# Routed experts computed on sorted 128-row tiles in place of all experts for all tokens

## The chip, the cores and the metric

The kernel runs on one core of a Trainium2 chip. The metric is the device time of one execution in microseconds. Several executions are timed and one is profiled: the profile gives, for each instruction on each engine, its start, its length and what ended the wait before it.

## The reference

x has 2048 tokens of 256 features. Two layers act on it. Layer 0 is attention (16 heads of 16 over all 2048 tokens) and a mixture of experts; layer 1 is a small attention over the first 32 tokens' scores and one binarised 256x256 product. Each of the four sub-blocks is a LayerNorm, a modulation and a gated residual. The part that the change concerns is the mixture of experts:

```python
    x = hidden_states.reshape(-1, h)                      # 2048 x 256
    probs = softmax(x @ router_w.T)                       # 8 experts
    topk_w, topk_idx = top_k(probs, 2)
    topk_w = topk_w / sum(topk_w)
    combine = zeros((T, 8)).at[arange(T)[:, None], topk_idx].add(topk_w)
    for gw, uw, dw, ce in zip(gate_w, up_w, down_w, combine.T):   # 256x176, 256x176, 176x256
        moe_out += ce[:, None] * (silu(x @ gw) * (x @ uw) @ dw)
    shared = silu(x @ s_gate_w + s_gate_b) * (x @ s_up_w + s_up_b) @ s_down_w + s_down_b   # 352 wide
    return moe_out + shared
```

Only two of the eight weights `ce` of a token are not zero.

## The kernel before

Five engines run streams of their own, in the order in which their instructions are written, and wait on semaphores. Every product in the mixture of experts is made of three passes over numbers split in a rounded high part and a rest (fp32r): high by high, high by low, low by high. Products of layer 1 and all transposes are in full fp32.

First come the LayerNorm and the projections. Then attention runs as 16 units (`unit`, L519) of 16 key tiles each: a chunk of 512 queries and a group of four heads. Beside the last two units run the second LayerNorm of chunks 0 to 2, its transposes (`turn1`, L634) and the router (`logits` L642, `router` L1322). Chunk 3 follows inside the first chunk of the next stage.

The mixture of experts (`chunk`, L743, L1060, L1400) computes every expert for every token. The 8x176 expert columns and the 352 shared columns lie side by side: 1760 columns, NI = 14 tiles of up to 128. For each of four chunks of 512 tokens and each of the 14 tiles, a step does the following. PE makes gate and up products (`hidden`, L719, 6 matmuls of 512 columns each, L725). For the 11 expert tiles it also spreads the combine weights over 128 rows with a selector (L760). ACT takes Silu (L1067), DVE multiplies by up and by the combine weight (L1409, L1414), ACT rounds (L1075), DVE makes the rest (L1416), and PE makes 12 down matmuls of 256 columns (`down`, L701, L713), which sum over all 14 tiles in two PSUM banks. DVE multiplies the sum by the gate row in `gate_sums` (L1424), and Pool adds it to x (L1848). The layer 1 work of chunk c-1 runs beside the steps of chunk c (`beside_second`, `beside_rest`): LayerNorm on DVE and Pool, transposes, products in `l1_attend` (L855) and `l1_feed` (L884), and adds on DVE (`add_product`, L1499). Chunk 3's layer 1 work is the end of the kernel, in two halves of 256 tokens (L923 to L950, L1609 to L1670). PE is in strict order, so everything beside a step lengthens it by what PE spends on it.

SP issues nearly all DMAs: weights of the experts are loaded during attention (`load_gate_up`, L326), outputs at the end. Pool issues none.

## Time and profile before

| | us |
|---|---|
| median of 3 runs | 1183.8 (1178.45 to 1184.11) |
| profiled execution | 1180.42 |
| its span, first to last instruction | 1178.6 |
| PE busy in the span | 1090.2 (92%) |
| DVE, ACT, POOL busy | 885.8 (75%), 666.9 (57%), 245.6 (21%) |
| granted TensorE clock, mean | 0.968 of full speed |

The page divides the span in 40 slices and gives each engine's busy share, then names the chain of work that ended last. It is read first for the order of the stages, then stage by stage: an engine that is busy all the time in a stage is what a change has to relieve there, and the chain of waits in it says whether another one interrupts it.

### The profile page before, as it was taken

The page shows a single profiled execution, that of the slowest core. Times are in us where ns is not written, and L with a number is a line of the kernel's source. Part 1 is how long each engine was busy: PE and PEld are TensorE (multiplying, and loading weights), DVE is VectorE, ACT ScalarE, POOL GpSimd, SP SyncE. Part 2 cuts the span into 40 slices and gives each one's busy share as a digit, 9 for nine tenths or more (in the row PEclk, how much of TensorE's full clock was granted, in tenths as well). Part 3 has the DMA queues.
Part 4 walks back from the last instruction along what each step waited for, and adds up shares of the span by engine and source line. Part 5 has one row for each costly group of instructions (what it writes and reads, how often), then busy time and mean ns, then how long its engine had stood idle before and what let it go on. Part 6 is the DMA issues. An engine that isn't in the chain of part 4 may idle for free.

```text
span 1178.6 us, 18705 instructions
## 1 busy us (share of the span) xinstructions
PE 1090.2 (92%) x6130; PEld 576.0 (49%) x6130; DVE 885.8 (75%) x1113; ACT 666.9 (57%) x1253; POOL 245.6 (21%) x284
## 2 busy tenths in 40 slices
PE   4977999999989999998999999999989999999985
PEld 3533433333333334333333333333477788888874
DVE  5568788888878888887888888885576775666565
ACT  0212577777767777776777777777652223222321
POOL 2033845000001003000000001212130132313323
PEclk9889599999999999999999999999898999999997
DMA  7799000020000000000000000003010000000001
GB/s 166 212 132 177 20 14 2 15 76 1 14 16 1 14 15 1 14 11 6 15 2 14 15 1 15 1 2 124 4 52 1 18 1 1 19 1 5 14 0 36
DMA packets 27559, 36.75 MB, mean 31 GB/s; under 512 B 5632, under 2 KB 18528, under 8 KB 26720
## 3 DMA queue, kind: packets, MB, share of 16 engines
q1 hardware_dynamic: 24256, 34.12, 12.1%
q10 hardware_dynamic: 3232, 1.60, 0.7%
q8 instruction: 54, 0.88, 0.3%
q14 instruction: 17, 0.14, 0.0%
HBM read 24.70 MB, written 10.49 MB: 30 GB/s over the span
## 4 chain that ended last, share of the span: by engine, by line
PE 72%; ACT 12%; DVE 7%; issue 6%; DMA 1%; ACTq 1%; SPq 1%; POOL 0%; DVEq 0%; POOLq 0%
PE ps L589 21%; PE ps L545 18%; PE ps L725 11%; ACT prob L1040 10%; PE ps L713 6%; PE ps L510 4%; DVE mxp L1262 3%; PE ps L450 3%; PE ps L461 1%; PE ps L653 1%; DMA kst<-k_parts 1%; PE ps L884 1%; PE ps L855 1%; PE ps L582 1%; PE ps L939 1%
## 5 line engine op out<-in xcount | busy, mean ns | idle before, releaser
L1262 DVE TENSOR_REDUCE mxp<-ps 128x2 f32<-128x1024 f32 x512 | 603.3, 1221 | 122.2 <-PE ps L510 119.5
L1040 ACT ACTIVATE prob<-ps 128x512 f32<-128x512 f32 x1024 | 530.6, 603 | 172.9 <-PE ps L545 172.4
L545 PE MATMUL ps<-qst,kst 50*128 50x512 f32 x1024 | 366.2, 456 | 31.8 <-ACT nm L995 14.1
L545 PEld LDWEIGHTS ps<-qst,kst 50*128 50x128 f32 x1024 | 167.0, 190 | 335.3 <-ACT prob L1040 280.1
L510 PE MATMUL ps<-kst,qst 48*128 48x512 f32 x1024 | 303.6, 449 | 17.2 <-DVE mxp L1262 8.5
L589 PE MATMUL ps<-prob,vp 128*32 128x512 f32 x2048 | 280.9, 621 | 0.1
L510 PEld LDWEIGHTS ps<-kst,qst 48*128 48x128 f32 x1024 | 133.9, 189 | 53.1 <-DVE mxp L1262 25.2
L1075 ACT ACTIVATE hid_hi<-hid 128x512 fp32r<-128x512 f32 (+1 forms) x56 | 35.4, 632 | 132.4 <-DVE hid L1414 103.1
L1744 POOL TENSOR_TENSOR att_u<-o_tm,rec 128x256 f32<-128x256 f32 x16 | 9.9, 622 | 370.6 <-DVE rec L1271 370.5
L1409 DVE SCALAR_TENSOR_TENSOR hid<-ps,bu,sig 128x512 f32<-128x512 f32 (+1 forms) x56 | 41.8, 747 | 48.8 <-PE ps L725 38.9
L589 PEld LDWEIGHTS ps<-prob,vp 128*32 128x32 f32 x2048 | 40.7, 109 | 68.0 <-ACT prob L1040 39.6
L1416 DVE TENSOR_TENSOR hid_lo<-hid,hid_hi 128x512 fp32r<-128x512 f32 (+1 forms) x56 | 43.0, 769 | 39.9 <-ACT hid_hi L1075 39.9
L1067 ACT ACTIVATE sig<-ps,bg 128x512 f32<-128x512 f32 (+1 forms) x56 | 38.4, 685 | 60.9 <-PE ps L725 60.9
L725 PE MATMUL ps<-hT_hi,wu_hi 128*128 128x512 f32 (+3 forms) x112 | 44.4, 397 | 0.9 <-DVE wu_lo L1391 0.9
L725 PE MATMUL ps<-hT_hi,wg_hi 128*128 128x512 f32 (+3 forms) x112 | 44.9, 401 | 0.0
L713 PE MATMUL ps<-wd_hi,hid_hi 128*128 128x256 f32 (+1 forms) x224 | 43.7, 318 | 1.3 <-ACT hid_hi L1075 0.9
L725 PE MATMUL ps<-hT_lo,wg_hi 128*128 128x512 f32 (+3 forms) x112 | 44.3, 396 | 0.0
L725 PE MATMUL ps<-hT_lo,wu_hi 128*128 128x512 f32 (+3 forms) x112 | 44.3, 396 | 0.0
L725 PE MATMUL ps<-hT_hi,wu_lo 128*128 128x512 f32 (+3 forms) x112 | 43.9, 392 | 0.0
L725 PE MATMUL ps<-hT_hi,wg_lo 128*128 128x512 f32 (+3 forms) x112 | 43.8, 391 | 0.0
L1718 POOL CAST nmp<-nm 16x128 fp32r<-16x128 f32 x16 | 4.6, 290 | 182.7 <-issue 166.4
L713 PE MATMUL ps<-wd_hi,hid_lo 128*128 128x256 f32 (+1 forms) x224 | 36.4, 285 | 0.0
(211 smaller groups left out, 1072.8 us busy)
## 6 DMA issues: line engine op xcount, KB each, us to landing
qst<-q_parts SPq DMA_DIRECT2D x96, 64.0 KB, 2.3
kst<-k_parts SPq DMA_DIRECT2D x24, 256.0 KB, 14.0
k_parts<-parts SPq DMA_DIRECT2D x8, 512.0 KB, 3.1
q_parts<-parts SPq DMA_DIRECT2D x8, 512.0 KB, 4.8
x<-x SPq DMA_DIRECT2D x4, 512.0 KB, 9.2
wmod_sb<-wmod ACTq DMA_DIRECT2D x3, 512.0 KB, 8.8
wmod_sb<-wmod SPq DMA_DIRECT2D x1, 1536.0 KB, 6.6
out<-x SPq DMA_DIRECT2D x3, 512.0 KB, 2.9
```

What stands on the lines that cost most here:

```text
L450: last = nc.tensor.matmul(ps[:, 4 + n % 2, :], w[:, k, P * ft:P * (ft + 1)], hT[:, k, CH * c:CH * (c + 1)], start=k == 0, stop=k == KT - 1)
L510: last = nc.tensor.matmul(ps[:, 2 * p + b, :], qst[rows, g, a, P * j:P * (j + 1)], kst[rows, GP * g + a, CH * m:CH * (m + 1)], start=True, ...
L545: nc.tensor.matmul(ps[:, bank, :], kst[rows, GP * g + k // 2, P * t:P * (t + 1)], qst[rows, g, k // 2, :], start=True, stop=True).then_inc ...
L589: last = nc.tensor.matmul(ps[VW * k:VW * (k + 1), 7, :], vp[:, t, G * g + k, :], prob[:, t % 2, k, :], start=t == 0, stop=t == MT - 1)
L713: last = nc.tensor.matmul(ps[:, 6 + j // 2, D * (j % 2):D * (j % 2 + 1)], a[0:rows, it % 2, P * j:P * (j + 1)], b[0:rows, it, :], start=it ...
L725: last = nc.tensor.matmul(ps[0:rows, b + it % 2, :], w[wp][:, k, P * it:P * it + rows], hT_pair(hp, k, c), start=m == 0, stop=m == 3 * KT - 1)
L1040: nc.scalar.activation(prob[:, t % 2, k, :], ps[:, banks[(G * t + k) % len(banks)], :], ACT.Exp, scale=DH ** -0.5).then_inc(p_s, 1)
L1067: nc.scalar.activation(sig[0:rows, it % 2, :], ps[0:rows, it % 2, :], ACT.Silu, bias=bg[0:rows, it:it + 1]).then_inc(sig_s, 1)
L1075: nc.scalar.activation(hid_hi[0:rows, it % 2, :], hid[0:rows, it % 2, :], ACT.Copy).then_inc(hid_hi_s, 1)
L1262: nc.vector.tensor_reduce(own, ps[:, 2 * p:2 * p + 2, :], AX.X, ALU.max).then_inc(mx_read, 1)
L1409: nc.vector.scalar_tensor_tensor(full, ps[0:rows, 2 + it % 2, :], bu[0:rows, it:it + 1], sig[0:rows, it % 2, :], ALU.add, ALU.mult).then_i ...
L1416: nc.vector.tensor_tensor(hid_lo[0:rows, it % 2, :], full, hid_hi[0:rows, it % 2, :].bitcast(F32), ALU.subtract).then_inc(hid_lo_s, 1)
```

## The change

The shared expert keeps the old form, with 3 tiles of its 352 columns for each of 4 chunks: 12 steps (`S_ROWS`, `ST` = 3). The routed experts are computed on tokens in the order of their experts:

- DVE ranks the probabilities, marks the two chosen experts, and PE counts with 0/1 matrices in bf16 how many earlier tokens chose each expert (`sort`, once for tokens 0 to 1535 and once for the last 512). DVE turns the counts into one slot for each of a token's two choices, with each expert's slots rounded up to whole tiles of 128 (`sort`, `shares`).
- There are always 31 + 15 = 46 tiles, filled or not. Empty slots are zeros: SP writes zeros to the slots in HBM during attention.
- Pool makes the tokens in rows (`tokens_by_row`, two 1024-column operations a chunk) and writes each of 16 row tiles twice to HBM by an indirect DMA with 128 row numbers (`place`, 24 + 8 DMAs).
- For each tile: SP loads it, PE transposes it (2), makes gate and up in one product of 352 columns (6 matmuls), transposes the hidden tile (2) and makes the down product (6 matmuls of 256 columns). PE reads the tile's expert from SBUF into a register (`value_load`), and the weights are addressed with it. ACT has four instructions for a tile and DVE three. SP stores the result to HBM.
- Pool fetches results for each token by 32 indirect DMAs with four buffers (`gather`). DVE multiplies each by its weight and adds it to x (`gathered`).
- The gate row of layer 0 is multiplied into the down weights, the two gate rows of layer 1 and its residual into the right hand matrices (`att3`, `bwT`), so that a product is added to x straight from PSUM by one operation in place of two (`add_product`).
- Layer 1 of chunks 0 and 1 begins beside tiles 37 to 47. What is left of chunks 0 to 2, and all of chunk 3, follows behind the tiles. Products alternate between two PSUM banks.
- The weights have a new layout. Pool splits the shared and the down weights during attention. ACT, Pool and DVE split gate and up in four pieces (`gate_up_rest`) behind it. In the kernel before, the up weights' and part of the down weights' splits stood there.

The core of the diff:

```diff
+PARTS = ((0, NT - TPC), (NT - TPC, TPC))
+TILES = [2 * n + E - 1 for _, n in PARTS]
+TS = sum(TILES)
...
+            def load_tile(i):
+                n, rows = tile_rows(i)
+                sp.wait_ge(placed[n], 16 * 2 * PARTS[n][1])
+                if i < XB:
+                    sp.wait_ge(u_ps, ST * (NC - 1))
+                else:
+                    sp.wait_ge(tin_ps, i - XB + 1)
+                sp.dma_start(xg[:, i % XB, :], x_slots[n][rows, :]).then_inc(xg_in[i % XB], 16)
...
+            def store_tile(i):
+                n, rows = tile_rows(i)
+                sp.wait_ge(yv_s, i + 1)
+                sp.dma_start(y_slots[n][rows, :], ysb[:, i % YB, :]).then_inc(y_out[i % YB], 16)
...
+            for i in range(TS + 2):
+                if i >= 2:
+                    store_tile(i - 2)
+                if i + 6 < TS:
+                    load_tile(i + 6)
...
+                    pe.wait_ge(slot_s, part)
+                flat = chosen[:].rearrange("p t e -> p (t e)")
+                nc.tensor.matmul(ps[:, 4, 0:E * tiles], before_bf[:], flat[:, E * t0:E * (t0 + tiles)], start=True, stop=False,
+                                 skip_group_check=True)
+                for t in range(tiles):
+                    last = nc.tensor.matmul(ps[:, 4, E * (t + 1):E * (tiles + 1)].rearrange("p (t e) -> p t e", e=E), ones_bf[:],
+                                            chosen[:, t0 + t, :].unsqueeze(1).to_broadcast([P, tiles - t, E]),
+                                            start=False, stop=t == tiles - 1, skip_group_check=True)
+                last.then_inc(sort_ps, 1)
...
+            def turn_in(i):
+                pe.wait_ge(xg_in[i % XB], 16 * (i // XB + 1))
+                if i:
+                    pe.wait_ge(tl_s, i)
+                for ft in range(KT):
+                    last = nc.tensor.transpose(ps[:, 0, P * ft:P * (ft + 1)], xg[:, i % XB, P * ft:P * (ft + 1)], ident[:])
+                last.then_inc(tin_ps, 1)
...
+            def gate_up(i, e):
+                pe.wait_ge(th_s, i + 1)
+                pe.wait_ge(tl_s, i + 1)
+                if i >= 2:
+                    pe.wait_ge(hdt_s, i - 1)
+                n = 0
+                for k in range(KT):
+                    for a, b in ((th, gu_hi), (th, gu_lo), (tl, gu_hi)):
+                        last = nc.tensor.matmul(ps[:, 2 + i % 2, 0:2 * I], a[:, i % 2, k, :],
+                                                b[:].rearrange("p e k n i -> p (e k n i)")[:, bass.ds(e * GW + k * 2 * I, 2 * I)],
+                                                start=n == 0, stop=n == 3 * KT - 1)
+                        n += 1
+                last.then_inc(gu_ps, 1)
...
+            def turn_hidden(i):
+                pe.wait_ge(hdt_s, i + 1)
+                if i:
+                    pe.wait_ge(hl_s, i)
                 else:
-                    pe.wait_ge(h_full_s, KT * (NC - 1) + 1)
-                turn(ln(1, NC - 1), ft, 5)
-
-            def logits3(c):
...
+            def down_tile(i, e):
+                pe.wait_ge(hh_s, i + 1)
+                pe.wait_ge(hl_s, i + 1)
+                if i:
+                    pe.wait_ge(yv_s, i)
+                m = 0
+                for n in range(2):
+                    for a, b in ((hh, d_hi), (hh, d_lo), (hl, d_hi)):
+                        last = nc.tensor.matmul(ps[:, 6, 0:D], a[:, i % 2, n, :],
+                                                b[:].rearrange("p e n d -> p (e n d)")[:, bass.ds(e * (2 * D) + n * D, D)],
+                                                start=m == 0, stop=m == 5)
+                        m += 1
+                last.then_inc(d_ps, 1)
...
+            def l1_product(d, right, done):
+                for half, bank in enumerate((1, 5)):
+                    for i in range(2):
+                        j = 2 * half + i
+                        for k in range(KT):
+                            last = nc.tensor.matmul(ps[:, bank, D * i:D * (i + 1)], hTc[d % 2][:, k, P * j:P * (j + 1)],
+                                                    right[:, k, :], start=k == 0, stop=k == KT - 1)
+                    last.then_inc(done, 1)
...
+            for i in range(TS + 2):
+                if i == TILES[0]:
+                    pe.wait_ge(owner_s, 2)
+                if i < TS:
+                    expert[i] = nc.tensor.value_load(owner[0:1, i:i + 1], min_val=0, max_val=E - 1)
+                    gate_up(i, expert[i])
+                if 1 <= i <= TS:
+                    turn_hidden(i - 1)
+                if i + 2 < TS:
+                    turn_in(i + 2)
+                if i >= 2:
+                    if i == 2:
+                        pe.wait_ge(y_read, NC)
+                    down_tile(i - 2, expert[i - 2])
+                beside_tile(i)
...
+            pe.wait_ge(za_s, 4)
+            l1_turn(3, 0)
+            l1_feed(0)
+            pe.wait_ge(f_s, 2)
+            l1_turn(2, 2)
+            l1_attend(2)
+            pe.wait_ge(za_s, 6)
+            l1_turn(3, 1)
+            l1_feed(1)
...
+            def input_rounded(i):
+                act.wait_ge(tin_ps, i + 1)
+                if i >= 2:
+                    act.wait_ge(gu_ps, i - 1)
...
+            def gate_tile(i):
+                act.wait_ge(gu_ps, i + 1)
+                if i >= 2:
+                    act.wait_ge(hdt_s, i - 1)
...
+            def leave_tile(i):
+                act.wait_ge(d_ps, i + 1)
+                if i >= YB:
+                    act.wait_ge(y_out[i % YB], 16 * (i // YB))
+                nc.scalar.activation(ysb[:, i % YB, :], ps[:, 6, 0:D], ACT.Copy).then_inc(yv_s, 1)
...
+            def beside_shared(n):
+                if n == 0:
+                    dve.wait_ge(pv_s, MT * (NU - 1))
+                    sort(0)
+                    shares(2)
+                if n and n % ST == 0:
+                    add_shared(n // ST - 1)
+                if n == 1:
+                    dve.wait_ge(att_s, NU)
+                    statistics(1, NC - 1)
+                if n == 2:
+                    normalise(1, NC - 1)
+                    gate_up_rest(2)
+                if n == 3:
+                    gate_up_rest(3)
+                if n in (4, 5):
+                    halves(NC - 1, n - 4, 5)
+                if n == 7:
+                    dve.wait_ge(pv_s, MT * NU)
+                    router(NC - 1, 5, 0)
+                if n == 9:
+                    sort(1)
+                    shares(NC - 1)
+            for n in range(ST * NC):
...
+            def input_rest(i):
+                dve.wait_ge(th_s, i + 1)
+                nc.vector.tensor_tensor(tl[:, i % 2].rearrange("p k n -> p (k n)"), ps[:, 0, 0:D],
+                                        th[:, i % 2].rearrange("p k n -> p (k n)").bitcast(F32), ALU.subtract).then_inc(tl_s, 1)
...
+            def gated_tile(i):
+                dve.wait_ge(sgt_s, i + 1)
+                if i >= 2:
+                    dve.wait_ge(ht_ps, i - 1)
+                nc.vector.tensor_tensor(hdt[:, i % 2, :], ps[:, 2 + i % 2, I:2 * I], sgt[:, i % 2, :], ALU.mult).then_inc(hdt_s, 1)
...
+            def gathered(d, tiles):
+                dve.wait_ge(xsd_s, d + 1)
+                for j in tiles:
+                    for k in range(2):
+                        m = gather_of(d, j, k)
+                        dve.wait_ge(yg_in[m % 4], 16 * (m // 4 + 1))
+                        if k:
+                            dve.wait_ge(yg_used, m)
+                        t = TPC * d + j
+                        nc.vector.scalar_tensor_tensor(x[:, t, :], yg[:, m % 4, :], share[:, t, k:k + 1], x[:, t, :],
+                                                       ALU.mult, ALU.add).then_inc(yg_used, 1)
+                dve.wait_ge(yg_used, m + 1)
...
+                    gathered(0, (0, 1))
+                if i == 38:
+                    gathered(0, (2, 3))
+                    statistics(2, 0)
+                if i == 39:
+                    normalise(2, 0)
+                if i == 40:
+                    first_tokens()
+                    gated_identity()
+                if i == 41:
+                    leave_uw()
+                    gathered(1, (0, 1))
+                if i == 42:
+                    gathered(1, (2, 3))
+                    statistics(2, 1)
+                if i == 43:
+                    attention_right()
+                    normalise(2, 1)
+                if i == 44:
+                    leave_xa()
+                if i == 45:
+                    attend(0)
+                    statistics(3, 0)
+                if i == 46:
+                    gathered(2, (0, 1))
+                    normalise(3, 0)
+                if i == 47:
+                    gathered(2, (2, 3))
+                    statistics(2, 2)
+                    attend(1)
...
+            def place(part, tiles):
+                pool.wait_ge(slot_s, part + 1)
+                pool.wait_ge(htm_s, 2 * (NC - 1 + part))
+                pool.wait_ge(zero_in, 16 * ZERO_DMAS)
+                for t in tiles:
+                    for k in range(2):
+                        nc.gpsimd.indirect_dma_start(
+                            x_slots[part], bass.IndirectOffsetOnAxis(ap=slots[:, PARTS[part][0] + t, k:k + 1], axis=0),
+                            h_tm[part][:, t, :], None).then_inc(placed[part], 16)
...
+            def gather(d, tiles):
+                part = 0 if d < NC - 1 else 1
+                for b in range(YB):
+                    pool.wait_ge(y_out[b], 16 * len([i for i in range(sum(TILES[:part + 1])) if i % YB == b]))
+                for j in tiles:
+                    for k in range(2):
+                        m = gather_of(d, j, k)
+                        if m >= 4:
+                            pool.wait_ge(yg_used, m - 3)
+                        nc.gpsimd.indirect_dma_start(
+                            yg[:, m % 4, :], None, y_slots[part],
+                            bass.IndirectOffsetOnAxis(ap=slots[:, TPC * d + j, k:k + 1], axis=0)).then_inc(yg_in[m % 4], 16)
```

## Rows read from the trace of the kernel before

**Rows 1.** Busy time of each engine by stretch; the columns are in the first line.

```profile
core 0: us, PE busy (x) PEld busy (x) DVE busy (x) ACT busy (x) POOL busy (x), PEclk, DMA share, GB/s
0.00:850.50 850.50, 782.24 (x4472) 324.38 (x4472) 675.69 (x734) 568.88 (x1106) 158.87 (x202) 0.97 0.17 38
850.50:1143.40 292.90, 288.71 (x1598) 237.39 (x1595) 187.84 (x337) 94.04 (x140) 75.66 (x69) 0.99 0.04 11
1143.40:1178.60 35.20, 19.22 (x66) 14.28 (x65) 22.29 (x43) 4.02 (x8) 11.09 (x13) 0.81 0.09 30
1149.00:1157.00 8.00, 5.33 (x17) 3.77 (x18) 4.88 (x10) 1.27 (x3) 2.02 (x2) 0.71 0.20 67
```

**Rows 2.** Chain that ended last, one step: start, length, engine, line.

```profile
1026.08 0.44 PE ps L631 x4
1026.52 1.43 PE ps L713 x12
1027.95 2.78 PE ps L725 x12
1030.72 0.23 PE ps L760
```

**Rows 3.** Same chain elsewhere: router logits, row products, layer 1 products.

```profile
841.20 2.77 PE ps L653 x24
906.91 1.72 PE ps L425 x4
968.93 1.73 PE ps L855 x8
```

**Rows 4.** Groups by shape, 850 to 1142 us: count, busy us, mean ns of one.

```profile
L1094 ACT ACTIVATE wd_hi<-wd_raw 96x256 fp32r<-96x256 f32 x1 | 0.4, 399 | 0.0
L1206 DVE SCALAR_TENSOR_TENSOR rows<-mrow 128x256 f32<-128x256 f32 x2 | 0.9, 426 | 0.1
L1333 DVE TENSOR_TENSOR pr<-pr,r4b 128x32 f32<-128x32 f32 x1 | 0.2, 191 | 0.0
L1503 DVE TENSOR_TENSOR yt<-ps,rows 128x512 f32<-128x512 f32 x9 | 6.2, 685 | 0.3 <-issue 0.3
L1830 POOL TENSOR_TENSOR wd_lo<-wd_raw,wd_hi 128x1280 fp32r<-128x1280 f32 x1 | 3.0, 2997 | 4.0 <-ACT wd_hi L1094 4.0
L1697 POOL TENSOR_TENSOR rs<-veps,m 128x4 f32<-128x4 f32 x7 | 7.3, 1039 | 0.6
```

**Rows 5.** One LayerNorm in the timeline: start, length of all, engine, line.

```profile
821.92 1.40 DVE L1160 BATCH_NORM_STATS2 bn_st<-x 128x6 f32<-128x256 f32 x4
823.35 0.38 DVE L1167 BATCH_NORM_AGGREGATE mv<-bn_st 128x2 f32<-128x6 f32 x4
1154.18 1.38 DVE L1625 TENSOR_SCALAR xh<-x,mv,rs 128x256 f32<-128x256 f32 x4
```

**Rows 6.** SP's DMA issues: ns min/median/max; then median us from issue to landing.

```profile
L314 SPq DMA_DIRECT2D qst<-q_parts x96: 308/423/1634, 46.1 to 712.3; - x96
qst<-q_parts SPq DMA_DIRECT2D x96, 64.0 KB, 2.3
```

**Rows 7.** Timeline of the end: layer 1 products, modulation and the last stores.

```profile
1143.48 1.89 PE L884 MATMUL ps<-bwT,hTc 128*128 128x256 f32 x8
1149.17 3.55 PE L884 MATMUL ps<-bwT,hTc 128*128 128x256 f32 x8 [3.80 <-DVE yt L1503]
1155.06 1.58 PE L929 MATMUL ps<-ident,xh 128*128 128x128 f32 x8 [2.35 <-DVE xh L1625]
1174.06 2.35 SPq L408 DMA_DIRECT2D out<-x  x2
```

**Rows 8.** Timeline: DVE and Pool operations on two SBUF operands, alone and together.

```profile
1155.47 0.69 DVE L1655 TENSOR_TENSOR sig<-xh,rows 128x512 f32<-128x512 f32 x1
1155.69 1.59 POOL L1890 TENSOR_TENSOR sig<-xh,rows 128x512 f32<-128x512 f32 x1 [5.98 <-issue]
1156.20 1.64 DVE L1657 TENSOR_TENSOR sig<-sig,rows 128x512 f32<-128x512 f32 x1
```

**Rows 9.** PE's register operations in the loop over chunks: count, ns min/median/max.

```profile
L725 PEldq FUSED_REGOPS  x8: 46/56/65, 999.6 to 1070.5; - x8
```

More of the change, by code:

```diff
@@ L160, in little @@
+        xh1 = at("xh1", [P, TPC, D], F32, qp_reg + 17408)
+        zero = at("zero", [P, D], F32, qp_reg + 21504)
+        small = [qp_reg + 22528]
         def little(name, shape, dt=F32):
@@ L717, in down @@
+                                                start=s == 0 and part == 0 and j % 2 == 0,
+                                                stop=s == ST - 1 and part == 2, skip_group_check=True)
                 last.then_inc(hid_used, 1)
-            def hidden(w, b, c, it):
-                rows = P if it < NI - 1 else LAST
-                m = 0
-                for k in range(KT):
-                    for wp, hp in PASSES:
-                        last = nc.tensor.matmul(ps[0:rows, b + it % 2, :], w[wp][:, k, P * it:P * it + rows],
-                                                hT_pair(hp, k, c), start=m == 0, stop=m == 3 * KT - 1)
-                        m += 1
-                return last
@@ L909, in l1_last_steps, with l1_xa @@
-            def l1_last_steps(c, it):
-                if it in (7, 9):
-                    l1_attend(c, (it - 7) // 2)
-                if it in (12, 13):
-                    l1_turn(c, 3, it - 12)
-            chunk(1, beside_second)
-            with pe.Fori(2, NC) as c:
-                chunk(c, beside_rest)
-            down(NC * NI - 1, NI - 1, None)
-            for half in range(2):
-                l1_feed(NC - 1, half)
+            def l1_xa():
+                pe.wait_ge(att_z, 1)
+                for k in range(KT):
+                    last = nc.tensor.matmul(ps[0:DX, 7, 0:D], hTc[0][:, k, 0:DX], att[:, k, :], start=k == 0, stop=k == KT - 1)
+                last.then_inc(xa_ps, 1)
@@ L1135, in _ @@
+            l1_modulate(2, 2)
+            l1_modulate(3, 1)
+            for h in range(2):
+                end_modulate(0, h)
+            l1_modulate(3, 2)
+            for h in range(2):
+                end_modulate(1, h)
         @block.vector
@@ L1349, in router @@
[L1349 to L1355 removed]
+                nc.vector.tensor_tensor(cmp_a[:], other, own, ALU.is_gt)
@@ L1665, in _ @@
+            normalise(2, 2)
+            statistics(3, 1)
+            feed(0)
+            normalise(3, 1)
+            gathered(3, (0, 1))
+            end_statistics(0, 0)
+            attend(2)
+            statistics(3, 2)
+            gathered(3, (2, 3))
+            end_statistics(0, 1)
+            feed(1)
+            end_normalise(0, 0)
+            end_normalise(0, 1)
+            normalise(3, 2)
+            for h in range(2):
+                end_add(h, za_ps, za_s)
                 end_statistics(1, h)
+            feed(2)
```

1395 lines of the change are left out of this document (695 added, 700 removed).

## Prediction

> **What bounds the kernel now.** I first cut the span into stages [rows 1]. Attention and all before it take 850.5 us, the mixture of experts 292.9, and the end of layer 1 35.2; together 1178.6. In the middle stage PE is busy 288.7 of 292.9 us at a granted clock of 0.99, DVE 188 and ACT 94. Then I read the chain of waits inside that stage. It is PE alone: for one step of an expert tile 2.78 us for 12 gate and up matmuls, 0.23 for spreading the weights, 1.43 for 12 down matmuls, and whatever stands beside it, such as 0.44 for four transposes [rows 2]. So the stage is a sum of PE's work. 44 expert steps take 44 x 4.44 = 195 us, 12 shared steps 12 x 4.21 = 50.5, and the other 47 us are router and layer 1 products and some waits. In the last stage no engine is full (PE 19, DVE 22 of 35 us); there the length is a chain of handoffs, and the clock falls, to 0.71 in the stretch shown [rows 1].
>
> **Part 1: what goes.** The 195 us of expert steps. They compute 16 x 8 = 128 pairs of a 128-token tile and an expert. The change always computes 46 such tiles, full or not. The number is fixed in the code, so that part cannot fail to happen.
>
> **Part 2: what a tile costs PE.** Per matmul with its weight load the chain shows 2.78/12 = 0.232 us for 512 columns and 1.43/12 = 0.119 for 256 [rows 2], and 2.77/24 = 0.115 for 8 columns [rows 3]. Below 256 columns the weight load sets the pace, above it the columns do. 352 columns then come to 0.119 + 96/256 x 0.113 = 0.161. A transpose is 0.44/4 = 0.11. A tile is 6 x 0.161 + 6 x 0.119 + 4 x 0.11 = 2.12 us. 46 tiles are 98 us, half of what goes.
>
> Can the others keep up? ACT's four instructions are like the 256-column rounding at 0.40 us [rows 4], so 1.5 us a tile. DVE's three have 256, 176 and 256 columns with one operand in PSUM; 0.43 for 256 [rows 4] gives 1.2. Each step of the pipeline has about one tile's time of slack, because PE turns tile i+2 and makes the down product of tile i-2 beside tile i. So PE sets the pace. PE's register work is new: about 8 address operations a tile at 0.056 us [rows 9], and one read from SBUF that the trace does not show. If the queue runs ahead of the matmuls both are free; the far end is one DMA's landing, 2.3 us [rows 6], though this is no DMA. I take 2.25 us a tile, near the free end, because in the loop over chunks such operations delayed nothing.
>
> **Part 3: up to the end of the shared steps.** In the last attention unit the second chunk's router waits for an exponential at key tile 12 and the third chunk's transposes are due at 13, with 7 us of DVE work between: +2 us (-3 to +5), to 852.5. The shared stage is PE's 50.5, two sets of logits 2 x 2.77 [rows 3], transposes, the last of attention and about 18 counting matmuls, together 60 us. The DVE chain is new there. Router, sort and shares of the first part are some 25 dependent small operations at 0.19 to 0.43 us [rows 4], 8 us in one piece where DVE is wanted every 4.2: 5 us late. Chunk 3's LayerNorm waits for Pool, which now stands behind two splits of 1408 columns (2.997/1280 x 1408 = 3.3 us each [rows 4]) and its first indirect DMA: 4 us late. 60 + 9 = 69 (63 to 80), to 921.5.
>
> **Part 4: Pool's indirect DMAs.** The trace has none. The ends are an issue on SP, 0.31 us at the least, and a whole small DMA to landing, 2.3 us [rows 6]. I take 1.2, because Pool's operation on four columns takes 1.04 [rows 4]: fixed cost rules there too. The 24 placing DMAs run from about 872: 24 x 1.2, with chunk 3's Pool work and two landings, end near 910, so the first tile is in before 921.5. They stay hidden up to 1.7 us each. SP's zero stores and weight loads lie under attention, where the DMA engines are busy 0.17 of the time [rows 1]; SP has a whole unit, over 40 us, between its loads of q. If that cover is gone each costs its 2.3 us.
>
> **Part 5: tiles 0 to 36.** 37 x 2.25 = 83.3, start 1.5, the three row products 3 x 1.72 = 5.2 [rows 3], one set of transposes 0.4, and lumps of DVE work that exceed its slack (columns, binarise) 4: 94.4, to 1016. At 2.12 it is 5 less.
>
> **Part 6: tiles 37 to 47, with layer 1 of chunks 0 and 1.** Now DVE is late. Nine tiles at 1.2 are 10.7; 24 gathered operations with three operands at 0.46 are 11; four statistics at 1.8 and three normalisations at 1.38 [rows 5] are 11.3; the rest (first tokens, right hand matrix, adds from PSUM at 0.69) is 9: 42 us, against 20 of PE for the tiles and 12 for products. DVE waits inside it as well. The gather has four buffers, and the second half of each chunk's gather starts only when DVE has used the first: 4 x 1.2 + 2.3 landing, less one tile, is 5 us, three times, a little of it shared: 12. LayerNorm and product handoffs add 3. Queued behind DVE's wait are the hidden and input rests of the tiles, and PE waits for those. 57 us (46 at 0.4 us an issue, 71 at 2.1), to 1073.
>
> **Part 7: the end.** Feed of chunk 0, attend of chunk 2 and feed of chunk 1 follow one another, each with transposes 0.9, modulation, two product halves of 1.73 [rows 3] and an add: 6.5 us. At the low clock eight such matmuls take 3.55 instead of 1.89 [rows 7]; two slow halves add 3.5. Together 23. Chunk 3's own chain from its first transposes to the end took 1178.6 - 1155.1 = 23.5 [rows 7]. It now has chunk 2's feed inside (+6) and four DVE operations of 0.69 less (-2). So 51 (42 to 62), and the span ends at 1124. Outside the span lie 1180.4 - 1178.6 = 1.8 us.
>
> **The sum** against the profiled 1180.4: +2, the shared and tile stages 292.9 -> 220.5, the end 35.2 -> 51, so 1126; I say **1125 us**. The median of the runs is 3.4 above the profiled one and their spread 5.7, which I leave in the range.
>
> **A rule against it.** Two operations of 512 columns on two SBUF operands show 0.69 on DVE alone and 1.64 when Pool works beside it [rows 8]. The Trainium skill, page "SBUF — State Buffer", section "Who interferes with whom", says that DVE and Pool share a port pair as an exclusive lock, and that a DVE operation with two SBUF inputs contends with Pool's reads; the trace agrees. By that page's sentence that a DMA issued by Pool cannot write its descriptors during DVE's two-port modes, the gathers would also stand behind each normalisation.
>
> **Rivals.**
> 1. *Slower: Pool's indirect DMAs are dear.* At 3 us each, placing 24 ends 32 us later than the shared steps, 24 gathers with six landings make stage 6 92 us in place of 57, and the last 8 add 14: 1125 + 81 = 1206. It decides from about 2.6 us. Against it: Pool's small operation takes 1.04. For it: no row of such a DMA.
> 2. *The tile pace is 3.0*, from register reads or handoffs that do not overlap: 46 x 0.75, less 6 hidden under DVE: 1153. At the far end of 2.3 us a tile it would be slower than before.
> 3. *The shared port.* If each of the 32 gathered operations and the adds beside them wait some 1 us as in rows 8 (1.64 - 0.69), it is 1155.
> 4. *Few stalls.* 2.12 a tile (-5), 0.5 us an issue (-12), shared stage without waits (-6), a shorter end (-7): 1095.
> 5. Clock: PE busy 60% of stage 6 may lose half its clock as in the end [rows 1]; its 32 us would become up to 45, still under DVE's 57. No case of its own.
>
> **How the numbers follow.** Forecast 0.45, rival 1 0.09, rival 2 0.18 (0.02 of it at its far end), rival 3 0.12, rival 4 0.16. About 0.5%, 6 us, is what a measurement of this kernel can tell from no change. Faster takes in all but rival 1, the far end of 2 and some mixtures of 1, 2 and 3: 0.85 faster, 0.04 same, 0.11 slower. The range of 8 in 10 reaches from below rival 4 past rivals 2 and 3 together with part of the end's bound: 1088 to 1176.
>
> **What would show each step.** Expert matmuls of 352 columns 0.16 us apart and 2.1 to 2.4 us from tile to tile on PE at full clock between about 922 and 1016. DVE at work nearly throughout the stretch of tiles 37 to 47, with waits for the gather in the second half of each chunk. Pool's indirect issues 1 to 1.5 us apart, the first tile's load not late. An end of about 50 us with the clock near 0.8. The prediction is wrong if PE's gaps between tiles exceed 0.5 us, if the shared stage ends after 940, or if Pool's queue is what the first tile waits for.

## The result, and the profile of the changed kernel

The changed kernel takes 1144.7 us (median of 4, 1139.93 to 1148.26) against 1183.95 before: ratio 0.966, interval 0.960 to 0.973. Medians and ratios here leave out runs over 1.5% above the fastest of the same kernel, one of g1 and one of h2 below. The forecast was 1125 with a range of 1088 to 1176, so direction and size held, and the point was 20 us too low. The profiled execution took 1143.2 us with a span of 1141.5. Its stages, in the columns of [rows 1], cut where the shared stage's first product, the first tile, DVE's first gathered operation and the end of the last tile stage stand:

```profile
core 0: us, PE busy (x) PEld busy (x) DVE busy (x) ACT busy (x) POOL busy (x), PEclk, DMA share, GB/s
848.87:933.43 84.56, 64.49 (x383) 52.41 (x379) 52.91 (x115) 27.53 (x39) 57.87 (x46) 0.92 0.22 77
933.43:1037.20 103.77, 94.54 (x612) 85.19 (x613) 57.73 (x144) 47.10 (x149) 13.42 (x8) 0.95 0.34 104
1037.20:1094.00 56.80, 38.93 (x199) 31.95 (x198) 37.52 (x110) 14.81 (x39) 26.27 (x29) 0.85 0.27 80
1094.00:1141.50 47.50, 32.90 (x144) 26.42 (x144) 28.86 (x73) 9.98 (x16) 24.85 (x26) 0.89 0.21 67
```

What was one stretch with PE busy 288.7 of 292.9 us, and a short end [rows 1], is now four stretches, and PE is full in none. By the forecast's clock the first tile should have started at 921.5, tile 37 at 1016, the end stage at 1073, the end come at 1124. Measured: 933.4 (12 later), 1037.2 (9 more), 1094.0 (nothing more), 1141.5 (3.5 less). So the miss lies in the shared stage and in tiles 0 to 36. What PE waited for in the shared stage (engine, line, releaser: us in total, times, longest):

```profile
PE ps L794 <- ACT hid_hi L1188: 8.9, 2, 7.6
PE ps L850 <- DVE tl L1612: 4.6, 1, 4.6
PE ps L794 <- DVE x L1567: 2.9, 1, 2.9
PE ps L807 <- DVE chosen L1480: 1.6, 1, 1.6
```

With four more of 0.2 to 0.7 these are 19.9 us, where the sum had 9. (In three kernels below that have the same shared stage, e1, e3 and e4, they are 13.4 to 15.2.) The 7.6 us wait belongs to the sort on DVE, beside Pool's splits of the weights (timeline: start, length, engine, line, operation):

```profile
863.04 6.36 POOL L2047 TENSOR_TENSOR gu_lo<-gu_raw,gu_hi 128x1408 fp32r<-128x1408 f32 x2
...
863.36 0.25 DVE L1509 SCALAR_TENSOR_TENSOR place<-first,ps 128x96 f32<-128x96 f32 x1
863.65 2.73 DVE L1512 SCALAR_TENSOR_TENSOR own<-rank,place 128x96 f32<-128x96 f32 x1
866.42 0.25 DVE L1513 TENSOR_REDUCE slot<-own 128x12 f32<-128x96 f32 x1
866.71 2.80 DVE L1512 SCALAR_TENSOR_TENSOR own<-rank,place 128x96 f32<-128x96 f32 x1
...
874.02 1.23 PE L794 MATMUL ps<-sd_hi,hid_hi 128*128 128x256 f32 x4 [7.56 <-ACT hid_hi L1188]
```

Operations of one size take 0.25 us with one operand in PSUM, and 2.7 to 2.8 with both in SBUF while a Pool instruction of 3.2 us runs. The same picture stands at tile 22, where the weight of layer 1 is binarised, and PE's distance from tile to tile is 9.3 us instead of 2.3:

```profile
986.45 9.56 POOL L2077 TENSOR_TENSOR x<-x,gsd 128x1024 f32<-128x1024 f32 x4 [55.97 <-DVE gb L1646]
...
988.90 2.57 DVE L1652 TENSOR_SCALAR bw<-w_sb 128x512 f32<-128x512 f32 x1
991.51 4.66 DVE L1654 TENSOR_SCALAR bw<-bw,alpha 128x256 f32<-128x256 f32 x2
```

A second kind of wait has no releaser. The profile calls a wait "remote" where no recorded event explains its end. The kernel before has none on ACT or DVE in these stages; the changed one has six, 14.9 us together. One of them, with PE's rows in front of it:

```profile
1028.80 0.32 PE L878 MATMUL ps<-gu_hi,tl 128*128 x1
1028.96 0.38 PE L892 MATMUL ps<-ident,hdt 128*88 128x128 f32 x2
...
1029.62 0.94 POOL L2089 DMA_INDIRECT yg<-y_slots,slots  x1 [0.30 <-issue]
...
1031.52 0.32 ACT L1207 ACTIVATE sgt<-ps 128x176 f32<-128x176 f32 x1 [2.51 <-remote]
```

The gate and up product ends at 1029.1 and ACT, which usually starts 0.36 us after its last matmul's start, starts 2.7 us after it. PE itself went on. The record of the counter that this product raises has the update at 1031.50, so the signal was late, not ACT. Each of the six waits begins among Pool's indirect DMAs and ends at most 1.5 us behind the last of a row. The theory for the experiments: the missing 20 us are (P) DVE operations locked out by whole Pool instructions, (H) signals of PE held back while indirect DMAs are issued, and (R) PE's register read. The rivals: DVE's lumps themselves, the gather's waits, and ordinary DMA traffic.

### The profile page after: what moved, and what is told of

The parts are those of the page before. It is cut to its first block, busy times and chain, and to the rows that moved or that the text cites. A ratio compares the mean times of both kernels' runs of the same rounds, so it can differ in the third digit from the quotient of the medians.

```text
span 1141.5 us, 18834 instructions
## 1 busy us (share of the span) xinstructions
PE 1012.0 (89%) x5772; PEld 518.3 (45%) x5772; DVE 848.2 (74%) x1158; ACT 668.3 (59%) x1346; POOL 301.3 (26%) x325
## 3 DMA queue, kind: packets, MB, share of 16 engines
q0 software_dynamic: 3072, 8.39, 2.4%
## 4 chain that ended last, share of the span: by engine, by line
PE 63%; ACT 12%; DVE 11%; issue 7%; DMA 3%; another core or an unknown queue 1%; POOL 1%; ACTq 1%; SPq 1%; DVEq 0%; POOLq 0%
PE ps L675 21%; PE ps L631 19%; ACT prob L1154 10%; PE ps L596 4%; PE ps L878 3%; DVE mxp L1399 3%; PE ps L536 3%; PE ps L904 2%; PE ps L776 1%; PE ps L963 1%; DMA kst<-k_parts 1%; PE ps L547 1%; DMA yg<-y_slots,slots 1%; PE ps L717 1%
## 5 line engine op out<-in xcount | busy, mean ns | idle before, releaser
L2089 POOL DMA_INDIRECT yg<-y_slots,slots x32 | 32.2, 1005 | 52.9 <-DMA y_slots<-ysb 29.8
L1207 ACT ACTIVATE sgt<-ps 128x176 f32<-128x176 f32 x46 | 14.6, 318 | 47.8 <-PE ps L878 44.7
L878 PE MATMUL ps<-gu_hi,th 128*128 x92 | 35.8, 389 | 2.2 <-DVE tl L1612 0.8
L892 PE MATMUL ps<-ident,hdt 128*88 128x128 f32 x92 | 18.5, 284 | 17.2 <-DVE hl L1623 17.2
L904 PE MATMUL ps<-d_hi,hh 88*128 x92 | 31.2, 339 | 2.5 <-issue 2.5
L878 PE MATMUL ps<-gu_hi,tl 128*128 x92 | 30.7, 333 | 0.0
L878 PE MATMUL ps<-gu_lo,th 128*128 x92 | 30.7, 333 | 0.0
L1315 DVE TENSOR_SCALAR xh<-x,mv,rs 128x256 f32<-128x256 f32 x56 | 21.7, 449 | 11.7 <-POOL rs L1875 8.2
L1220 ACT ACTIVATE ysb<-ps 128x256 f32<-128x256 f32 x46 | 17.7, 385 | 20.8 <-PE ps L904 17.6
L1188 ACT ACTIVATE hid_hi<-hid 128x512 fp32r<-128x512 f32 (+1 forms) x12 | 7.6, 631 | 37.8 <-DVE hid L1601 30.3
L2057 POOL DMA_INDIRECT x_slots<-h_tmA,slots x24 | 26.7, 1111 | 7.8 <-issue 6.6
```

What stands on the lines that cost most here:

```text
L878: last = nc.tensor.matmul(ps[:, 2 + i % 2, 0:2 * I], a[:, i % 2, k, :], b[:].rearrange("p e k n i -> p (e k n i)")[:, bass.ds(e * GW + k * ...
L892: last = nc.tensor.transpose(ps[0:IH, 4, P * n:P * (n + 1)], hdt[:, i % 2, IH * n:IH * (n + 1)], ident[:])
L904: last = nc.tensor.matmul(ps[:, 6, 0:D], a[:, i % 2, n, :], b[:].rearrange("p e n d -> p (e n d)")[:, bass.ds(e * (2 * D) + n * D, D)], st ...
L1315: nc.vector.tensor_scalar(dst, x_cols(t), mean, rs, ALU.subtract, ALU.mult).then_inc(xh_s, 1)
L2057: nc.gpsimd.indirect_dma_start(x_slots[part], bass.IndirectOffsetOnAxis(ap=slots[:, PARTS[part][0] + t, k:k + 1], axis=0), h_tm[part][:, t ...
L2089: nc.gpsimd.indirect_dma_start(yg[:, m % 4, :], None, y_slots[part], bass.IndirectOffsetOnAxis(ap=slots[:, TPC * d + j, k:k + 1], axis=0)) ...
```

## The experiments

The attention part is the same code in all of them, and yet the shared stage's first product started between 847.0 and 861.7 us, so the whole times differ by more than most edits are worth. The lengths of the stages in the profiled runs are steadier: where an edit does not touch it, the shared stage took 82.7 to 84.6 us (e1, e3, e4 and the changed kernel), and the rest 206.8 to 210.0 (e2, f2, h1 and the changed kernel). They hide a trade: in those four PE waited 13.4 to 19.9 us in the shared stage, and its own work took 64.7 us where it waited longest and 68.2 to 70.2 in the others, at a granted clock of 0.92 and 0.86 to 0.89. The verdicts rest on the stages, and on single waits and distances; a difference of a stage under 3 us is not told apart. There is one profile of each kernel. The last column is the time as a share of the kernel before, which was timed anew beside each group of experiments (1183.95 to 1188.24 us). All lengths, us:

| kernel | shared stage | PE's waits in it | first tile to end | both | whole, median | ratio |
|---|---|---|---|---|---|---|
| changed | 84.6 | 19.9 | 208.1 | 292.6 | 1144.7 | 0.966 |
| e1, additions behind the binarising | 83.4 | 15.2 | 203.7 | 287.1 | 1144.4 | 0.965 |
| e2, splits in four pieces | 81.3 | 12.1 | 207.2 | 288.6 | 1150.1 | 0.973 |
| e3, eight gather buffers | 83.6 | 13.4 | 207.5 | 291.1 | 1148.4 | 0.969 |
| e4, fixed owner | 82.7 | 13.4 | 205.4 | 288.1 | 1139.1 | 0.963 |
| f1, plain DMAs on Pool | 78.5 | 11.5 | 196.8 | 275.2 | 1137.2 (one) | - |
| f2, SyncE places | 78.5 | 10.7 | 206.8 | 285.3 | 1134.1 (one) | - |
| f3, slower issues | 101.9 | 27.8 | 227.0 | 328.9 | 1181.3 (one) | - |
| g1, combined | 80.6 | 12.7 | 199.7 | 280.2 | 1137.4 | 0.960 |
| h1, placing spaced | 88.4 | 15.7 | 210.0 | 298.4 | 1150.7 | 0.966 |
| h2, g1 with placing spaced | 82.6 | 14.4 | 201.7 | 284.3 | 1137.2 | 0.960 |
| h3, h2 with gathers spaced | 83.7 | 13.6 | 205.6 | 289.3 | 1148.1 | 0.966 |
| i1, g1 with the read ahead | 82.1 | 13.1 | 196.5 | 278.6 | 1135.4 | 0.957 |

### Pool out of the binarising's way

```diff
                 pool.wait_ge(y_read, c + 1)
+                pool.wait_ge(bw_s, 1)
```

> Pool's four additions of the shared bias (4 x 2.39 us, 986.45 to 996.0 in the changed kernel) wait until DVE has the layer 1 weight binarised; nothing else changes. Theory P (the shared port: a DVE operation of this kind waits until Pool's running instruction is over): the three tensor_scalar of the binarising take 0.86 and twice 0.81 us as in the kernel before, not 2.57 and twice 2.33; the gap from tile to tile there falls from 9.3 us to 4 to 5; the whole is 4 to 6 us shorter, about 1139. Theory L (the DVE lump itself is the cost, five operations in one piece): the gap stays 7 us or more and the time 1144 to 1146.

```profile
998.87 0.43 DVE L1652 TENSOR_SCALAR bw<-w_sb 128x512 f32<-128x512 f32 x1
999.34 0.62 DVE L1654 TENSOR_SCALAR bw<-bw,alpha 128x256 f32<-128x256 f32 x2
```

The same three operations take 1.05 us in place of 7.2, faster even than the 0.86 and 0.81 us that the kernel before showed. The distance at tile 22 is 2.6 us where it was 9.3, below the 4 to 5 expected; one of 3.7 us stands at tile 19, where it was 2.2. From the first tile to the first gathered operation it is 6.1 us less, to the end 4.4. Theory P; the lump alone costs 0.3 us. The whole time does not show it (1144.4 against 1144.7). In the profiled run attention ended 9 us later; the other runs left no profile.

### The splits in pieces

```diff
-                nc.gpsimd.tensor_tensor(gu_lo[:, lo:hi]..., ALU.subtract).then_inc(gu_lo_s, 1)
...
+                for m in range(4):
+                    w = slice(n * m, n * (m + 1))
+                    last = nc.gpsimd.tensor_tensor(a[:, w], b[:, w], c[:, w].bitcast(F32), ALU.subtract)
+                last.then_inc(gu_lo_s, 1)
```

> Pool's two splits of 1408 columns in the shared stage are each made in four instructions of 352 columns. They still lie beside the sort's two scalar_tensor_tensor of 96 columns, which took 2.73 and 2.80 us in the changed kernel against 0.25 for operations of that size beside them. Theory P (the port is held for a whole Pool instruction, and DVE gets it between two of them): these two take at most 0.25 + 0.8 = 1.05 us, PE's stall before the second down product falls from 7.56 to about 4.5, and the shared stage is 3 us shorter. Theory B (Pool and DVE share bandwidth throughout its 6.4 us): they stay at 2.7, and the stage doesn't change.

```profile
872.39 7.51 POOL L2051 TENSOR_TENSOR gu_lo<-gu_raw,gu_hi 128x352 fp32r<-128x352 f32 x8
...
873.01 0.43 DVE L1512 SCALAR_TENSOR_TENSOR own<-rank,place 128x96 f32<-128x96 f32 x1
873.76 0.58 DVE L1512 SCALAR_TENSOR_TENSOR own<-rank,place 128x96 f32<-128x96 f32 x1
...
881.42 1.23 PE L794 MATMUL ps<-sd_hi,hid_hi 128*128 128x256 f32 x4 [3.55 <-ACT hid_hi L1188]
```

As theory P said, and more: 0.43 and 0.58 us, the stall 3.55 instead of 7.56, the stage 3.3 us shorter, though Pool works 1.2 us longer in all. What is held is at most one Pool instruction long. The two operations took 2.7 to 2.9 us in e3, e4 and f1 too, but the stall was 5.7, 5.6 and 7.6 there, so that the cut is worth 2 to 4 us of the stall, and of the stage 1.4 to 3.3.

### Eight gather buffers

```diff
-        yg = at("yg", [P, 4, D], F32, q_reg + 7168)
+        yg = at("yg", [P, 8, D], F32, q_reg + 7168)
...
-                        if m >= 4:
-                            pool.wait_ge(yg_used, m - 3)
+                        if m >= 8:
+                            pool.wait_ge(yg_used, m - 7)
```

> The gather has eight buffers and eight semaphores in place of four, so the second half of a chunk's gather no longer waits for DVE. The prediction's term for these waits is 12 us. If that is right, the stretch of tiles 37 to 47 falls from 57 us to 45 to 49 and the whole to about 1135. If Pool's issue pace rules (32 gathers 1.25 us apart, 10 us for a chunk, a third of the stretch) only chunk 0 gains: 3 to 5 us, 1140. If DVE's work is the bound and the waits lie beside work that is late anyway: under 2 us.

DVE's waits for the gather fall as meant (changed kernel, then this one: us in total, times, longest):

```profile
DVE x L1675 <- DMA yg<-y_slots,slots: 10.5, 12, 1.8
```

```profile
DVE x L1675 <- DMA yg<-y_slots,slots: 4.0, 4, 1.9
```

Still only 0.6 us is won. Eight indirect DMAs now stand in one row in front of tile 36, and the distance to tile 36 is 9.0 us where it was 4.1:

```profile
1045.95 0.38 ACT L1213 ACTIVATE hh<-ps 88x256 fp32r<-88x256 f32 x1 [1.12 <-remote]
...
1046.93 0.39 PE L892 MATMUL ps<-ident,hdt 128*88 128x128 f32 x2 [3.65 <-DVE hl L1623]
...
1048.07 0.38 ACT L1200 ACTIVATE th<-ps 128x256 fp32r<-128x256 f32 x1 [1.75 <-remote]
```

The three expectations missed what happened. From the first gathered operation on the kernel is 6.4 us shorter (97.9 for 104.3), but that operation comes 5.8 us later behind the first tile (109.6 for 103.8). The waits were real, and the remedy turned them into held signals: six waits without a releaser beside the tiles, 12.2 us, where the changed kernel has three of 5.5.

### The owner fixed

```diff
-                    expert[i] = nc.tensor.value_load(owner[0:1, i:i + 1], min_val=0, max_val=E - 1)
+                    expert[i] = i % E
```

> Each tile takes expert i mod 8, fixed in the code, in place of the one read from SBUF: PE's 46 register reads and the address operations go. The outputs are those of the wrong experts. If the reads are hidden in front of the matmuls, as the distance of 2.1 to 2.35 us from tile to tile in the changed kernel says, 0 to 2 us shorter. If they are what lies between 2.12 and the 2.25 of the sum: 46 x 0.13 = 6 us shorter. If they were what the tile pace hangs on (rival 2): over 10 us.

The first matmul of two tiles in a row, in the changed kernel and in this one:

```profile
1011.85 0.42 PE L878 MATMUL ps<-gu_hi,th 128*128 x1
...
1014.15 0.42 PE L878 MATMUL ps<-gu_hi,th 128*128 x1
```

```profile
970.12 0.33 PE L878 MATMUL ps<-gu_hi,th 128*128 128x352 f32 x1
...
972.23 0.33 PE L878 MATMUL ps<-gu_hi,th 128*128 128x352 f32 x1
```

The distance falls from 2.30 (tiles 24 to 34, median) or 2.39 (2 to 20) to 2.11 in both: the free end of the forecast, 2.12, to a hundredth. Tiles up to the first gathered operation take 5 us less (98.7 for 103.8), and half of it is given back later, at tiles 40 and 44, where PE waits for DVE. The middle reading (0.13 a tile) is nearest for the distance, at 0.2 to 0.3; of its gain 2.7 us are left, which is within what the stages can tell. The edit takes out the reads and the address operations together; which of them it is, the last experiment tells.

### What holds PE's signals: plain DMAs, another issuer, and distance

In f1 every indirect DMA becomes a plain one, in f2 only the placing ones, issued by SyncE:

```diff
-                        nc.gpsimd.indirect_dma_start(
-                            x_slots[part], bass.IndirectOffsetOnAxis(ap=slots[...], axis=0),
-                            h_tm[part][:, t, :], None).then_inc(placed[part], 16)
+                        nc.gpsimd.dma_start(x_slots[part][P * (2 * t + k):P * (2 * t + k + 1), :],
+                                            h_tm[part][:, t, :]).then_inc(placed[part], 16)
```

> All 64 of Pool's indirect DMAs become plain DMAs of the same 128 rows of 1 KB, still issued by Pool, to and from fixed rows, so that the routing is lost and the output is not the reference's. In the changed kernel PE's signals reach ACT and DVE 2.4 to 4.3 us late at some places, all inside stretches in which Pool issues these DMAs (ACT at 912.98 and 1031.52, DVE at 895.76 and 930.52). Theory H (the held signals belong to the indirect form): they go, the shared stage (84.6 us from its first product to the first tile) is 6 to 9 us shorter. Theory S (they belong to any DMA that Pool issues): they stay, and the stage is within 2 us. The price of an issue, 1.25 us, shows beside it: whether the list of rows or the DMA itself costs it.

> Only the 32 placing DMAs are changed: SyncE issues them as plain copies to fixed rows (routing lost), the gathers stay indirect on Pool. Theories H and S both expect that the shared stage loses all the late signals and is 6 to 9 us shorter than the 84.6 us, while those of the gathers stay, ACT's 2.5 us beside the first four gathers among them. If late signals in the shared stage stay, they come from the DMA traffic or from something else, and both fall.

f1 has no remote wait at all, f2 none before its gathers and one of 1.6 us beside them. The shared stage is 78.5 us in both, 4 to 6 us less than in the four kernels that have it as it was. Pool's queue moved 3072 packets and 8.39 MB in the changed kernel and in f1, so it is not the amount of traffic. f1's rows also follow one another in HBM where the routed ones are scattered; h1 to h3 below scatter them still. Pool's issues (ns min/median/max; first and last start), changed kernel and f1:

```profile
L2057 POOL DMA_INDIRECT x_slots<-h_tmA,slots x24: 959/963/2269, 870.3 to 910.5; - x24
L2089 POOL DMA_INDIRECT yg<-y_slots,slots x32: 945/950/1377, 1025.8 to 1111.2; - x32
```

```profile
L2057 POOL DMA_DIRECT2D x_slots<-h_tmA x24: 539/539/1367, 881.6 to 910.4; - x24
L2089 POOL DMA_DIRECT2D yg<-y_slots x32: 536/546/667, 1030.9 to 1104.2; - x32
```

With 0.30 us to the next, an indirect issue is 1.25 us, a plain one 0.54. What f1 gains behind the first tile, 11 us, is both effects and can't be split here. Next, a Pool operation with no use for the result goes before each DMA: in f3 one of 1.05 us (`slowed`) before all 64, in h1 one of 0.23 us (`space`) before the 32 placing ones:

```diff
+                        space()
                         nc.gpsimd.indirect_dma_start(
```

> A Pool operation of 1.05 us goes before each of the 64 indirect DMAs, so that each costs 2.3 us of Pool and not 1.25. This measures the slope of rival 1. By the prediction placing is hidden up to 1.7 us each: 24 x 0.6 = 14 us more in the shared stage, 24 x 1.05 = 25 less what lies beside DVE's work in the stretch of tiles 37 to 47, 5 at the end: 30 to 44 us in all. If Pool's issues are hidden better than that: under 20.

> The changed kernel with a Pool operation of 0.23 us before each of the 32 placing DMAs, and nothing else: they stand some 1.6 us apart, not 1.25. With 2.31 us between them no signal of PE came late, with plain copies neither. Theory D (density: signals are held only while these DMAs follow one another at 1.25 us): the late signals of the shared stage go, it falls from 84.6 us to 79 to 81 although Pool does more. Theory F (any indirect DMA can hold them; that none was held at 2.31 us was chance): late signals stay, and Pool's 24 x 0.35 = 8 us more leave the stage at 84 to 88.

f3 is 36.3 us longer, inside its 30 to 44, and its one run of 1181.3 is all but the time before. No remote wait is left in it. In h1 none is left in the shared stage, and the three beside its unspaced gathers stay. So theory D holds for the signals; the stage did not come as it said: 88.4 us. Pool's longer row of DMAs (1.5 to 2.8 us apart, some of the small operations took 0.8 to 1.4) makes the last chunk's input late, and PE waits 4.5 us for it where it waited for nothing. All its waits together are 15.7 us, still less than the 19.9 of the changed kernel. But its own work took 72.7 us where the four kernels with the stage as it was took 64.7 to 70.2, at a granted clock of 0.84. Why the clock was lower is open.

The label alone would mislead: e1 and e2 place as densely as the changed kernel and have no remote wait in the shared stage either. One wait of PE measures the holding in all kernels, the one before the second tile is turned, while the last placing DMAs go out. h1, then the changed kernel:

```profile
940.95 0.41 PE L852 MATMUL ps<-ident,xg 128*128 128x128 f32 x2 [1.74 <-DVE tl L1614]
```

```profile
932.22 0.66 PE L850 MATMUL ps<-ident,xg 128*128 128x128 f32 x2 [4.59 <-DVE tl L1612]
```

It is 1.74 us in all six kernels with plain or spaced placing (f1, f2, f3, h1, h2, h3), and 2.24 to 4.59 us in all seven with indirect DMAs 1.25 us apart. The records of PE's counters say the same. Counted as late is an update over 0.3 us behind the end of the last product that raises the counter. The shared stage has 11 of them in the changed kernel and 3 to 8 in the other six with dense placing, and none in the six. Counters that ACT, DVE and Pool raise are not late in any kernel up to the last tile. Beside the tiles f1 and f3 have none; h3, whose gathers stand 1.47 us apart, still has four, of 0.7 to 1.0 us, which its profile shows as ordinary waits, such as

```profile
1028.51 0.38 ACT L1222 ACTIVATE ysb<-ps 128x256 f32<-128x256 f32 x1 [1.04 <-PE ps L906]
```

So the form matters (plain or indirect), and the density: with 1.25 us between the DMAs waits of up to 4.4 us, with 1.5 signals on time or at most 1.0 us late, with 2.3 all on time. The spacing was always made with an operation of Pool and a wait for it, so distance and what fills it are not told apart, except that h3 and f3 both have them and differ. What inside the chip holds a counter's update is not shown.

### Put together

```diff
                     sort(0)
-                    shares(2)
...
                 if n == 3:
                     gate_up_rest(3)
+                    shares(2)
...
-                if i == 37:
+                if i == 34:
                     gathered(0, (0, 1))
...
+                pool.wait_ge(bw_s, 1)
```

The splits are in four pieces too, and each `beside_tile` entry from 37 on stands three lower on PE, ACT and DVE.

> Put together: Pool's additions wait for the binarising (as in e1, -6 in the tile stage), its two splits in four pieces (as in e2, -3), the shares of the third chunk three shared steps later (-1.7), and the whole layer 1 work beside the tiles, on PE, ACT and DVE, three tiles earlier (34 to 44 in place of 37 to 47). DVE has 1 us of slack a tile, so three tiles earlier is worth 3 to 6 us where DVE's work is the bound; nothing if the held signals and the gathers are. Sum 12 to 16 us under the changed kernel, 1129 to 1133; 1134 to 1138 if the last step gives nothing.

> The combined kernel (g1) with the placing DMAs spaced as in h1. Its shared stage was 80.6 us with one late signal of 4.1 us in it. By theory D that goes: 77 to 79, and the whole 2 to 4 us under g1, about 1136. By theory F nothing or 2 us more.

> As h2, with the 32 gathering DMAs spaced too. By theory D the late signals beside the tiles go (1.1, 1.8, 3.2 and 1.8 us in g1), while 24 gathers at 0.35 us more each cost up to 8 us where DVE waits for them: from -3 to +4 us against h2. By theory F +4 to +8.

g1 wins 12.4 us by its stages (4.0 and 8.4) and 7 by the medians: ratio to the kernel before 0.960 (0.955 to 0.965). Its parts alone gave 3.3 and 4.4, which leaves about 4 for the three tiles and 1 for the shares; neither was run alone. Spacing does not pay: by the stages h2 is 4 us over g1 and h3 9, though h3 has no remote wait; by the ratios h2 is no better and no worse (0.960 both), and h3 is 0.966. Theory D's gain did not come, as in h1. Last, the owner of the next tile is read behind the gate and up product instead of behind the down product:

```diff
-            expert = {}
+            expert = {0: nc.tensor.value_load(owner[0:1, 0:1], min_val=0, max_val=E - 1)}
...
+                if i + 1 < TS:
+                    expert[i + 1] = nc.tensor.value_load(owner[0:1, i + 1:i + 2], min_val=0, max_val=E - 1)
```

> The combined kernel (g1) with the expert of tile i+1 read right behind the gate and up product of tile i, not behind the down product of tile i-2; as many reads and address operations as before. With the expert fixed (e4) tiles came 2.11 us apart, with the read 2.30 to 2.38. If the 0.2 us are the matmul queue running dry because the read stands behind six short matmuls of 0.12 us, tiles come 2.11 to 2.2 apart, 5 to 8 us less in tiles 1 to 33, and the whole 3 to 6 us under g1. If PE's sequencer is simply busy for longer than the matmuls take (its total per tile is the bound), they stay at 2.3 and nothing changes.

Tiles 24 to 34 come 2.11 us apart, as with a fixed owner, tiles 2 to 20 2.26 apart. The part behind the first tile is 3.1 us shorter than in g1, the whole 2.0 (3 to 6 expected), and the ratios' intervals overlap; the distance is what shows the gain. This is the fastest kernel of those that keep the routing: 1135.4 us (1129.78 to 1137.43), ratio 0.957 (0.953 to 0.961), 9 us under the changed kernel.

## Why the prediction held, and where it was short

**Part 1 and the per-matmul prices** were right: the expert steps are gone from the code, and 46 tiles stand in their place, at 2.11 us each when no read is in the way (e4, i1) against 2.12 forecast from 256, 512 and 8 columns [rows 2, 3].

**Part 2, the register read.** "The free end" was the wrong side by a little: 2.30 to 2.39 and not 2.25. The reason given, that such operations delayed nothing in the loop over chunks [rows 9], was taken from matmuls of 0.23 us. Six matmuls of 0.12 us did not cover a read of 0.35 us and its checks of 0.17; six of 0.16 did (i1). Over 37 tiles this is 3 us of the miss.

**Part 3, the shared stage** is the step that failed: 84.6 us for 69, of which 3.6 came back because the stage began at 848.9 and not at 852.5, so that the first tile was 12 late. PE's work was 4.7 longer (64.7 for 60, at 0.92 granted where the kernel before had 0.99 [rows 1]), and the stalls were 19.9 and not 9. Of these the sort took 7.6, of which the lock explains 2 to 4 (e2). Held signals, with Pool's own queue behind them, took 4 to 6: f1 and f2 are that much shorter. The 8 us for the sort's 25 operations were priced from rows of DVE alone [rows 4], though the next term of the same sum was Pool's splits of 3.3 us beside them.

**Part 4, the indirect DMA**: 1.25 us against 1.2. The nearest row was Pool's 1.04 us operation, as argued. Landing was 2.8 and not 2.3 us. Rival 1's slope was 45 us for each us; f3 gives 36.3 / 1.05 = 35, so that the change would stop paying at 1.25 + 39/35 = 2.4 us an issue, where 2.6 was said.

**Part 5, tiles 0 to 36**, was 9 us short: the read 3, and the lumps of DVE work, 4 in the sum. They measure 7.0 at tile 22, 1.1 behind it and 1.6 at tile 18, 9.7 together; the lock is 4 to 6 of it (e1). The first four gathers held a signal for another 2 before tile 36, and the three row products cost 1.1 instead of 1.72 each, 2 back.

**Parts 6 and 7**: 57 us as forecast, and 47.5 for 51. That part 6 came out to a fifth of a us is partly luck. Its terms are 37.5 us of DVE work (42 said), 10.0 of gather waits (12) and 5.5 of waits for a tile's gate, in which late signals take part and which the sum did not have. DVE was busy 37.5 of 56.8 us, not nearly throughout as the sign said. The term of 12 was near in size, but e3 shows that more buffers do not buy it back: the 6.4 us won there were lost before it.

None of the three signs of being wrong showed: the pace was 0.3 us over 2.11 at most outside the lumps and row products, the shared stage ended at 933.4 and not after 940, and PE turned the first tile at 925.4 without waiting for its load.

**Rivals.** Rival 2's read was real at 0.2 to 0.3 us a tile, not 0.75. Rival 3 named the right mechanism at the wrong place: the 32 gathered operations took 0.48 us in the median, with Pool's DMA issues beside them, and only one took 2.40, beside Pool's own addition of 2.35 us:

```profile
1113.69 2.35 POOL L2096 TENSOR_TENSOR x<-x,gb 128x1024 f32<-128x1024 f32 x1
1113.91 2.40 DVE L1675 SCALAR_TENSOR_TENSOR x<-yg,share,x 128x256 f32<-128x256 f32 x1 [0.49 <-DMA yg<-y_slots,slots]
```

The lock fell on the sort and on the binarising instead. The section "Who interferes with whom" of "SBUF — State Buffer" in the Trainium skill also says that `tensor_scalar` in a two-port mode blocks against Pool for a whole instruction, which the 0.43 us against 2.57 agree with; priced at every Pool operation of the new schedule it would have pointed at both places. That the gathers stand behind each normalisation did not show: the issue at 1048.99, beside one, took 1.14 us against 0.95. Rival 4's short stalls did not come. Against the held signals stood no row: the kernel before issues no DMA from Pool.

## What to carry to other kernels

Before DVE work is moved beside Pool work, list for each long Pool instruction which DVE operations with two SBUF operands or of the fast scalar form can fall into it, and cut it into pieces or put a wait in front of it. The gain of one such line here was 4 us. Treat a row of indirect DMAs as something that other engines notice, beyond Pool's own 1.25 us each: do not put it beside a tight pipeline, and do not remove the pauses in it before looking. And read a register behind the longest queued matmuls, not behind the shortest.

## What had not been expected of the hardware

- ACT and DVE waited up to 4.4 us for PE's signals while Pool issued indirect DMAs 1.25 us apart. The signals were at most 1.0 us late with 1.5 us between the DMAs, and not late with plain ones (0.54 us apart) or with 2.3 us between them. PE's own matmuls went on.
- A `tensor_scalar` of 512 fp32 columns from SBUF to SBUF took 0.43 us alone, 0.86 in the kernel before and 2.57 beside Pool's long operations.
- Identical attention code ended up to 14.6 us apart between profiled runs. A whole time is then a poor judge of an edit in a later stage.
